# Key-tile slots in a gated cross-attention kernel: which maxima pair, value product or chunk stands behind which group of scores

## What is computed

```
x = x + tanh(g_xattn[0]) * attn0(layernorm(x), ctx, ctx, mask)
x = x + tanh(g_ffn[0])   * moe0(layernorm(x))         # 64 experts, grouped top-8, one shared expert
x = x + tanh(g_xattn[1]) * attn1(layernorm(x), ctx, ctx, energy)
x = x + tanh(g_ffn[1])   * moe1(layernorm(x))         # 8 experts, top-2

attn(q, k, v): 16 heads of width 8
  scores = einsum('bhqd,bhkd->bhqk', q, k) / sqrt(8)  # layer 0: masked
  out    = einsum('bhqk,bhkd->bhqd', softmax(scores), v) @ Wo + bo   # layer 1: softmax * gate of the key
```

## Time and profile before

| | |
|---|---|
| median of 3 runs | 1145.09 us (1144.63 to 1146.0) |
| the profiled execution | 1145.07 us, its span 1143.2 us |
| mean granted TensorE clock | 0.937 |
| busy: TensorE matmul, weight load | 85%, 61% of the span |
| busy: VectorE, ScalarE, GpSimd | 67%, 51%, 31% |
| attention of layer 0 | from about 65 to 450 us of the span |
| attention of layer 1 | from about 665 to 1000 us |

### The profile page before, as it was taken

How to read it: one execution, slowest core, us unless ns; L and a number is a source line. 1 busy time by engine, 2 the same in 40 slices (tenths; PEclk the granted TensorE clock), 3 DMA queues, 4 the chain that set the end, 5 groups by cost and what they waited for, 6 DMA issues and landing times.

```text
span 1143.2 us, 24455 instructions
## 1 busy us (share of the span) xinstructions
PE 969.1 (85%) x9740; PEld 696.8 (61%) x9740; DVE 761.8 (67%) x1459; ACT 586.3 (51%) x1194; POOL 351.6 (31%) x278
## 2 busy tenths in 40 slices
PE   4589999999999989579997788888988988860997
PEld 2256666666666666468885456656665656540986
DVE  7976766666666664659997975665655655240996
ACT  2035555555555566346664146666556566650664
POOL 6701121303122110047774704134133142000674
PEclk8879999999999999679999889999999999875999
DMA  6630303214040400075650632241340330005662
GB/s 165 119 66 28 79 27 80 66 41 106 3 103 1 107 1 2 8 211 169 167 168 18 148 75 51 56 106 32 75 105 28 79 80 28 2 4 85 181 166 61
DMA packets 48088, 88.52 MB, mean 77 GB/s; under 512 B 21154, under 2 KB 31558, under 8 KB 47974
## 3 DMA queue, kind: packets, MB, share of 16 engines
q1 hardware_dynamic: 47974, 86.96, 31.7%
HBM read 47.24 MB, written 1.75 MB: 43 GB/s over the span
## 4 chain that ended last, share of the span: by engine, by line
PE 59%; DVE 14%; ACT 11%; POOL 6%; issue 5%; DMA 4%; SPq 1%; POOLq 0%; DVEq 0%; ACTq 0%
PE ps L1139 17%; PE po L1159 14%; PE pm L1110 13%; ACT probs L844 8%; POOL tmpf L768 6%; PE ps L1142 5%; PE pc L1091 3%; PE pc L1078 3%; DVE vaug L530 2%; DVE qsel L521 2%; ACT qsel L928 2%; DMA routing<-vaug 2%; DVE mx_part L412 1%; DVE junk L417 1%; DMA wts<-in_experts 1%
## 5 line engine op out<-in xcount | busy, mean ns | idle before, releaser
L844 ACT ACTIVATE probs<-ps 121x400 f32<-121x400 f32 (+1 forms) x768 | 363.8, 504 | 302.1 <-PE ps L1142 173.3
L1139 PE MATMUL ps<-qst,kst 128*121 128x400 f32 (+1 forms) x768 | 298.5, 420 | 60.6 <-ACT probs L844 57.9
L1110 PE MATMUL pm<-khi,qbd 128*100 128x482 f32 (+1 forms) x696 | 257.7, 453 | 21.8 <-DVE mx_part L417 8.7
L412 DVE TENSOR_REDUCE mx_part<-pm 128x2 f32<-128x964 f32 (+1 forms) x160 | 180.4, 1134 | 104.5 <-PE pm L1110 104.4
L1139 PEld LDWEIGHTS ps<-qst,kst 128*121 128x121 f32 (+1 forms) x768 | 138.9, 184 | 182.1 <-ACT probs L844 126.4
L417 DVE CUSTOM_DVE_ANT_0 junk<-pm,negq 100x964 bf16<-100x964 f32 x128 | 146.7, 1160 | 77.7 <-PE pm L1110 76.6
L1244 PE MATMUL pm<-qsel,qst 128*128 128x400 f32 x660 | 159.4, 366 | 40.4 <-DVE qsel L521 36.8
L1159 PE MATMUL po<-probs,vaug 121*32 121x100 f32 x6144 | 173.6, 254 | 1.4 <-ACT probs L844 1.4
L1159 PEld LDWEIGHTS po<-probs,vaug 121*32 121x32 f32 x6144 | 130.8, 110 | 64.4 <-issue 45.2
L1244 PEld LDWEIGHTS pm<-qsel,qst 128*128 128x128 f32 x660 | 123.6, 197 | 58.9 <-DVE qsel L521 58.1
L1110 PEld LDWEIGHTS pm<-khi,qbd 128*100 128x100 f32 (+1 forms) x696 | 118.5, 184 | 66.7 <-DVE mx_part L412 20.5
(11 more groups left out here) (176 smaller groups left out, 959.3 us busy)
## 6 DMA issues: line engine op xcount, KB each, us to landing
kst<-khi SPq DMA_DIRECT2D x128, 180.5 KB, 3.9
wb<-routing SPq DMA_DIRECT2D x66, 200.0 KB, 3.6
ctxT<-in_ctxT SPq DMA_DIRECT2D x16, 722.0 KB, 4.3
kst<-klo SPq DMA_DIRECT2D x64, 180.5 KB, 3.9
wts<-in_experts SPq DMA_DIRECT2D x55, 192.0 KB, 3.7
wb<-routing SPq DMA_DIRECT2D x22, 400.0 KB, 4.0
qsel<-qhi SPq DMA_DIRECT2D x16, 100.0 KB, 2.4
routing<-vaug SPq DMA_DIRECT2D x1, 1100.0 KB
```

The lines of the kernel that those rows point to most:

```text
L412: nc.vector.tensor_reduce(mx_part[0:rows, i * 3 + c:i * 3 + c + len(items)], bank[:, 0:len(items), :], AX, ALU.max).then_inc(s["max_taken" ...
L844: nc.scalar.activation(probs[t % 2][0:r, g * GQ:(g + 1) * GQ], ps[0:r, n % 2, 0:GQ], ACT.Exp, scale=SCALE).then_inc(s["probs_ready"], 1)
L1110: mm = nc.tensor.matmul(pm[0:rows, n % 2 * 2 + j, 0:MAX_W], qbd[b % 2][:, first:first + rows], khi[b % 2][:, lo:lo + MAX_W], start=True, s ...
L1139: mm = nc.tensor.matmul(ps[0:r, n % 2, 0:GQ], kst[b % 2][:, g, t * KEY_TILE:t * KEY_TILE + r], qst[b % 2][:, g * GQ:(g + 1) * GQ], start=T ...
```

## The change

In TensorE's slot the second group of scores now comes behind the first maxima pair (and behind `max_rows`), and `beside` goes from before the second pair to behind the fourth group of scores. In ScalarE's slot the fourth exponential goes ahead of the taking of a key or value chunk. No instruction is added or removed.

```
--- before.py
+++ after.py
@@ -876,11 +876,11 @@
                         exp_group(b, t, 2)
+                        exp_group(b, t, 3)
                         if b < B - 2 and 0 <= t - K_SLOT < 3:
                             k_high(b + 2, t - K_SLOT)
                         if b < B - 1 and 0 <= t - V_SLOT < V_CHUNKS:
                             v_raw(b + 1, t - V_SLOT)
-                        exp_group(b, t, 3)
@@ -1205,20 +1205,20 @@
                         scores(b, t, 0)
-                        scores(b, t, 1)
                         for u in here[0:1]:
                             max_unit(b + 1, u)
                         if b < B - 1 and t == ROW_SLOT:
                             max_rows(b + 1)
+                        scores(b, t, 1)
                         if t >= 1:
                             weigh(b, t - 1)
                         elif b >= 1:
                             weigh(b - 1, KEY_TILES - 1)
                         scores(b, t, 2)
-                        beside(b, t)
                         for u in here[1:2]:
                             max_unit(b + 1, u)
                         scores(b, t, 3)
+                        beside(b, t)
                         for u in here[2:]:
                             max_unit(b + 1, u)
```

## The result

The changed kernel takes 1075.21 us (median of 4 runs, 1072.04 to 1076.31) against 1145.55 us for the kernel before in the same session: a ratio of 0.9382, 95% interval 0.9359 to 0.9405. That is 70 us less, where 60 were forecast. The profiled execution took 1076.31 us, its span is 1074.5.

What follows compares the result with a forecast made beforehand. TensorE is busiest, stopped by score groups waiting for an exponential to free their PSUM bank. Layer 1 gives 39 us and layer 0 21, so 1145 - 60 = 1085 us; range 1072 to 1110.

Steps and rivals of the forecast that it cites:

- The wait before the second group is what the change removes: Both attentions: the second group's wait for the fourth group's exponential goes, 1085 us (1075 to 1096), chance 0.68.
- fall to about 10 each: Sign: score loads waiting for exponentials, 35.7 us in layer 0 and 52.0 in layer 1, fall to about 10 each.
- Which view to trust: Layer 0 waits: 35.7 us by weight loads, 14.1 by matmuls; forecast followed loads, matmul rows would give 53 in all.
- Layer 1, key and value intervals: Between value products with a chunk beside: key 4.10 to 3.44 us, gain 0.66; value 4.16 to 3.54, gain 0.62.
- Layer 1, nothing beside: Filler 0.77 us short of 1.16, second group still waits, value products follow at once: gain 0.38 us.
- Layer 1, slots 1 to 3: Intervals with short transposes and projection beside: gain 0.55 us each, between the key chunk and nothing beside cases.
- Layer 1, start of a batch: Slots 10, 11 and 0 together gain some 0.4 us, limited by `qbd` from GpSimd with 0.91 us in hand.
- Layer 0: Gains of 2.8 us in seven two-pair intervals, 0.1 in three three-pair ones, 0.1 in last two: 3.0 a batch, 21 total.
- ScalarE's swap costs nothing, and without it the exponential stands behind the chunk: ScalarE queue, chunk copy behind fourth exponential: no cost; otherwise the exponential the second group wants stands behind the chunk.
- The maxima as the new wait: Rival: the wait returns elsewhere by half, pairs waiting for VectorE, 1115 us, chance 0.10; L1110 waits otherwise below 5 us.
- The last batches: Last batch of each layer: no maxima, so nothing to put between and a gain of 0.
- The seventh batch of layer 1: Layer 1's seventh batch, without key chunks: gain about 5.3 us, against 5.65 for a full batch.

Runs made afterwards that it cites:

- one half of it alone: Kernel before with only the second group of scores moved behind the first maxima pair and `max_rows`; 1097.20 us, ratio 0.9598.
- the three kernels with `qbd` early: GpSimd spreads the maxima queries one batch earlier, before the value chunks: on the changed kernel 1073.41 us, kernel before 1149.78, changed kernel with first pair before first group 1069.88.

## Why the prediction was right, and where its sizes were off

- **The wait before the second group is what the change removes.** Right. In slots with a chunk it is gone. With nothing beside in layer 1 a wait of the forecast's size is left, 0.41 us, but it stands before the first group, and the forecast had it before the second. The second group's load still sits where ScalarE puts it, 793.60 - 791.13 = 2.47 us behind the value products against 844.32 - 841.84 = 2.48 before, so the interval came out as worked out. That loads waiting for exponentials "fall to about 10 each" holds once the 0.15 us behind the value products are left out: 6.4 and 9.9.
- **Which view to trust.** The matmul rows left 14.1 us of waits in layer 0; the layer gave about 25. The first projection of layer 1, which comes between the two attentions, marks it; in the kernel before, by line:

```profile
L1030 PEld LDWEIGHTS pm<-ctxT,wk x8: 188/264/337, 10.5 to 618.8; 128*128 128x128 f32 x8
```

and in the changed kernel:

```profile
L1030 PEld LDWEIGHTS pm<-ctxT,wk x8: 187/264/338, 10.3 to 592.6; 128*128 128x128 f32 x8
```

  The last of them is 26 us earlier. The Trainium skill, "Perfetto Trace Analysis", section "Identifying the Most-Contended Engine", holds that matmul busy time does not measure the room that is left. The trace agrees: an engine busy to 96% by those rows still gave up 7% of its batch (50.39 to 46.76).
- **Layer 1, key and value intervals.** 3.44 and 3.54 were worked out, 3.43 and 3.50 came.
- **Layer 1, nothing beside.** 0.38 worked out, 3.28 to 2.90 came.
- **Layer 1, slots 1 to 3.** Mis-sized: 0.55 each was taken, 0.68, 0.55 and 0.65 came (3.73 to 3.05, 3.41 to 2.86, 3.51 to 2.86), 1.88 for 1.65. Moving the second group alone gave 0.44 in each of the three, moving the short piece alone 0.46, 0.12 and 0.22.
- **Layer 1, start of a batch.** The step was right, 0.53 us for the 0.4 taken, with the wait for GpSimd where it was put; without that wait the three intervals would have given 1.3.
- **Layer 0.** The largest miss: 3.0 us a batch taken, 3.63 came. The seven intervals with two pairs gave 3.4 us for 2.8, the three with three pairs 0.17 for 0.1, the last two 0.07 for 0.1. A value interval with two pairs became 4.18 us and not 4.33. I had every step at its full length; but the group behind the chunk takes 0.30 and not 0.40, and from the second group's load to the value products it is 0.66 and not 0.71, which makes the 0.15. Both can be read in the loads behind slot 7 of the changed kernel (193.55 to 193.85, and 194.24 to 194.90):

```profile
192.62 1.01 PEld L1091 LDWEIGHTS pc<-wv,ctxT 128*121 128x121 f32 x8
193.55 0.18 PEld L1139 LDWEIGHTS ps<-qst,kst 128*121 128x121 f32 x1
...
193.85 0.34 PEld L1110 LDWEIGHTS pm<-khi,qbd 128*100 128x100 f32 x2
194.24 0.18 PEld L1139 LDWEIGHTS ps<-qst,kst 128*121 128x121 f32 x1
...
194.90 0.67 PEld L1159 LDWEIGHTS po<-probs,vaug 121*32 121x32 f32 x32 [0.30 <-ACT probs L844]
```

- **ScalarE's swap costs nothing, and without it the exponential stands behind the chunk.** Right in both halves but for one interval: by itself it gives 0.31 us a batch in layer 1, some 2 us, and where it is left out 38 us are lost.
- **The maxima as the new wait.** Not in the change, whose pairs wait for VectorE for 1.6 us in layer 0 and not at all in layer 1 in the two windows above, below the 5 us named. But one half of it alone has it: 0.50 us in intervals with three pairs. The reason given against it, "the pair two before always has the value products in between, or a chunk", holds for the whole change only.
- **The last batches.** Put at nothing, since they have no maxima; 1.35 us came in layer 0 and 0.99 in layer 1. They do have pieces beside in slots 4 and 6, the first steps of the mixture of experts, and these moved too: the intervals behind them went from 3.46 to 2.97 and from 4.01 to 3.51 in layer 0, from 2.96 to 2.63 and from 3.50 to 2.82 in layer 1.
- **The seventh batch of layer 1.** "About 5.3" does not follow from the forecast's terms: with three plain intervals in place of the key intervals, 5.65 - 3 x (0.66 - 0.38) = 4.8. 6.0 came.

The 10 us between forecast and result can be laid out by batches. Layer 0 gave 24.4 us in its first seven batches for 21, and 1.35 in the last for 0. Layer 1 gave 30.9 in its five full batches for 28, some 12 in the first and the seventh together for 10.4, and 1.0 in the last for 0. The mechanism was right in both layers, and most terms came out a little larger than taken. The last batches differ by up to 1.8 us between executions of the same kernel, so their share is the least certain.

## What to carry to other kernels

Where one engine fills a pair of buffers that another empties, write down the distance from a fill to the moment its buffer is free again (here 1.16 to 1.32 us), and sum what the first engine has to do in between; only that sum counts, not whether each fill has a neighbour. Two moves that fill the same gap do not add up, and a move on the one engine wants its mirror on the other: a queue that names a later piece of work first throws the gain away. After such a change look where a third engine had less than a microsecond in hand, since all its due times came forward. And read the batches at the edges too: an edit that gains in every batch in the middle can lose as much in one place that comes once.

## What the chip showed that was not expected

Around the column-strip matmuls of the value products the weight loads sit idle each time. In the kernel before it is 0.33 to 0.37 us behind a maxima pair; in the changed kernel it is 0.30 to 0.32 behind a group of scores that ran on without a wait, and 0.19 to 0.27 behind one that had waited. On the way out it is 0.15 us, in 184 of the 192 sets of the changed kernel. Together that is about 0.46 us a slot. Whether this costs time isn't shown: by the matmul rows the neighbours touch, and what of it could be had back was not tried.

One instruction of VectorE, L385, which runs once, took 2.94 to 3.33 us in the three kernels with `qbd` early and 0.50 to 0.90 us in all the others. In every kernel GpSimd's four writes of `qst` (L695, 3.28 us together) run beside it. In the three it ends within 0.1 us of the last of the four, in the others at least 2 us before. Why moving `qbd`, which stands right behind these writes there, should matter was not tested. What shows is that such a move can lengthen another engine's instruction, and not only a wait: TensorE's maxima pair waited 3.53 us where it had waited 1.09.
